# A language-model tower on one core: first-stage buffers in another order, left row slots loaded one by one, bias scaling in eight pieces, first expert split in the state stage

## The reference

```python
h = 16 * sum(where(in_range_i, table_i[idx] @ proj_i.T, 0))   # 4 tables, 256 wide
n = layernorm(h)
x = silu(conv3(n @ w1.T + w1_b))            # depthwise, along the 128 positions
y = ssm(x)                                  # h = h*sigmoid(A) + x*B; y = C.h + D*x
h = h + (y * silu(n @ v1.T + v1_b)) @ w2.T + w2_b
f = layernorm(h)
shared = silu(f @ sw1 + sb1) * (f @ sw3 + sb3) @ sw2 + sb2
experts = sum over 2 hashed experts of gelu(f @ w1[e] + b1[e]) @ w2[e] + b2[e]
out = h + (shared + experts / 2) / 2
```

## Time and profile before

| | us |
|---|---|
| median of 3 runs (lowest, highest) | 440.92 (440.53, 441.39) |
| the profiled execution | 442.19 |
| its span, first to last instruction | 440.3 |
| PE busy | 400.3 (91%) |
| DVE, ACT, POOL busy | 272.8, 242.9, 212.6 |
| mean granted TensorE clock | 0.984 |

### The profile page before, as it was taken

The page is one execution under the profiler, slowest core; times in us unless marked ns, Lnnn a source line. Parts: engine busy times, 40 slices in busy tenths (PEclk is TensorE's granted clock), DMA queues, the critical chain, the costliest instruction groups (busy, mean ns, idle before and its releaser), DMA issues.

```text
span 440.3 us, 8454 instructions
## 1 busy us (share of the span) xinstructions
PE 400.3 (91%) x2880; PEld 352.4 (80%) x2880; DVE 272.8 (62%) x607; ACT 242.9 (55%) x435; POOL 212.6 (48%) x236
## 2 busy tenths in 40 slices
PE   3878999899997785899999999999999999998996
PEld 2767888788677774698898998988988988887885
DVE  6558998889756577565556465565564554655333
ACT  4576778778877345644544635635635535535442
POOL 6569999831006456557347237247247336333000
PEclk9999999999998988899999999999999999999999
DMA  2433121249699983100121111201201301100101
GB/s 63 143 111 131 49 61 56 69 129 308 196 302 297 237 293 104 67 0 20 59 68 48 44 55 48 58 38 48 85 10 48 95 0 48 48 0 0 49 0 48
DMA packets 32779, 38.86 MB, mean 88 GB/s; under 512 B 3461, under 2 KB 29027, under 8 KB 32624
## 3 DMA queue, kind: packets, MB, share of 16 engines
q1 hardware_dynamic: 29616, 32.99, 24.3%
q0 software_dynamic: 3136, 5.52, 4.2%
HBM read 34.56 MB, written 8.65 MB: 98 GB/s over the span
## 4 chain that ended last, share of the span: by engine, by line
PE 62%; DVE 16%; POOL 6%; ACT 6%; issue 5%; DMA 3%; SPq 1%; DVEq 0%; ACTq 0%; POOLq 0%
PE ps L1140 20%; PE ps L1141 19%; PE ps L1142 19%; DVE hid_lo L1073 3%; DMA h_in<-h_rows_dram 2%; DVE stat L951 2%; DVE catT_lo L944 1%; POOL bias_e L646 1%; POOL bias_e L645 1%; PE ps L1259 1%; PE ps L1178 1%; DVE act_out L1067 1%; ACT act_out L845 1%; DVE x_mid L1004 1%; DVE rstd L978 1%
## 5 line engine op out<-in xcount | busy, mean ns | idle before, releaser
L1073 DVE SCALAR_TENSOR_TENSOR hid_lo<-act_out,hid_hi 128x512 fp32r<-128x512 f32 x64 | 54.4, 851 | 57.5 <-ACT hid_hi L858 57.5
L845 ACT ACTIVATE act_out<-ps,vec 128x512 f32<-128x512 f32 x32 | 22.1, 689 | 90.3 <-PE ps L1142 90.3
L1067 DVE SCALAR_TENSOR_TENSOR act_out<-ps,vec,act_out 128x512 f32<-128x512 f32 x32 | 24.0, 751 | 55.5 <-ACT act_out L845 55.5
L675 POOL TENSOR_TENSOR h_sb<-h_sb,bias_e 128x256 f32<-128x256 f32 x32 | 24.5, 769 | 53.4 <-DVE h2n L964 53.4
L1141 PE MATMUL ps<-h2nT_lo,sw_hi 128*128 128x512 f32 x128 | 50.0, 391 | 0.0
L1142 PE MATMUL ps<-h2nT_hi,sw_lo 128*128 128x512 f32 x128 | 50.0, 391 | 0.0
L1140 PE MATMUL ps<-h2nT_hi,sw_hi 128*128 128x512 f32 x128 | 49.9, 390 | 0.0
L668 POOL TENSOR_TENSOR zc_lo<-v_sb,zc_hi 128x256 fp32r<-128x256 f32 x32 | 28.8, 903 | 34.4 <-ACT zc_hi L835 34.4
L849 ACT ACTIVATE act_out<-ps,vec 128x512 f32<-128x512 f32 x32 | 22.0, 689 | 40.5 <-PE ps L1142 40.3
L858 ACT ACTIVATE hid_hi<-act_out 128x512 fp32r<-128x512 f32 x64 | 39.7, 622 | 0.0
L528 POOL DMA_INDIRECT cat<-table_dram,x_ids x32 | 35.1, 1097 | 8.3 <-issue 5.9
(11 more groups left out here) (133 smaller groups left out, 1260.9 us busy)
## 6 DMA issues: line engine op xcount, KB each, us to landing
toep_l<-kernel_rows_dram SPq DMA_DIRECT2D x14, 512.0 KB, 9.3
toep_r<-kernel_rows_dram SPq DMA_DIRECT2D x12, 512.0 KB, 6.9
h_rows_dram<-h_ring SPq DMA_DIRECT2D x32, 128.0 KB, 1.8
h_in<-h_rows_dram SPq DMA_DIRECT2D x8, 512.0 KB, 4.4
stage<-w_e_dram POOLq DMA_DIRECT2D x7, 512.0 KB, 3.6
out_dram<-o_sb SPq DMA_DIRECT2D x7, 512.0 KB, 3.2
bias_e<-rows_dram SPq DMA_DIRECT2D x1, 1024.0 KB, 7.2
toep_r<-kernel_rows_dram SPq DMA_DIRECT2D x4, 256.0 KB, 7.9
```

What stands on the lines that cost most here:

```text
L675: nc.gpsimd.tensor_tensor(at, at, bias_e[:, bass.ds(e, 1), :].rearrange("p o c -> p (o c)"), ALU.add).then_inc(h2_biased, 1)
L845: nc.scalar.activation(act_out[:, n % 4, :], ps[bank][:, :], ACT.Silu, bias=vec[:, C_SB1 + j:C_SB1 + j + 1]).then_inc(act_done, 1)
L1067: nc.vector.scalar_tensor_tensor(act_out[:, n % 4, :], ps[bank + 1][:, :], vec[:, C_SB3 + j:C_SB3 + j + 1], act_out[:, n % 4, :], ALU.add, ...
L1073: nc.vector.scalar_tensor_tensor(hid_lo[:, n % 4, :], act_out[:, n % 4, :], 0.5 if kind == SHARED else 0.25, f32(hid_hi[:, n % 4, :]), ALU ...
```

## The change

The order of the buffers on the left side is changed: `cat`, `k_row`, `abar`, `catT`, `proj` now come first, so that each 8 KB slot for rows lies over buffers that are last used at different times. `ex0` and `ex1` change places, so that `ex1` and `stage` lie clear of what the first stage uses. SP's order in the last group is written out, with a wait for just what a slot needs; the bias loads move ahead; the first expert's load (`piece_in(1)`) goes ahead of load 10, its hi part (ACT) into q = 4 of the state stage, its lo part (POOL) ahead of the mixer bias. The bias scaling is cut into a row and eight pieces, each behind a `cat_hi` of group 1.

```diff
-    x_ids = sb(mem_a, "x_ids", [P, GROUPS, RES], I32, L)
-    mask = sb(mem_a, "mask", [P, GROUPS, RES], F32, L)
     cat = sb(mem_a, "cat", [P, RES, CAT], F32, L)
+    k_row = sb(mem_a, "k_row", [P, YLEN, 2, 2], F16, L)
+    abar = sb(mem_a, "abar", [P, 7, HALVES * STATES], F32, L)
     catT_hi = sb(mem_a, "catT_hi", [P, 2, KC, P], F32R, L)
     catT_lo = sb(mem_a, "catT_lo", [P, 2, KC, P], F32R, L)
-    hn = sb(mem_a, "hn", [P, 4, D], F32, L)
     proj_hi = sb(mem_a, "proj_hi", [P, KC, D], F32R, L)
     proj_lo = sb(mem_a, "proj_lo", [P, KC, D], F32R, L)
+    hn = sb(mem_a, "hn", [P, 4, D], F32, L)
     h_ring = sb(mem_a, "h_ring", [P, 4, D], F32, L)
...
+    x_ids = sb(mem_a, "x_ids", [P, GROUPS, RES], I32, L)
+    mask = sb(mem_a, "mask", [P, GROUPS, RES], F32, L)
...
-        sp.dma_start(bias_row[:, 0:1, :], bass.AP(rows.tensor, D, [[0, P], [D, 1], [1, D]])).then_inc(rows_in, 16)
-        sp.dma_start(bias_e[:, :, :], bass.AP(rows.tensor, 2 * D, [[0, P], [D, RES], [1, D]])).then_inc(rows_in, 16)
-        with sp.Fori(1, GROUPS - 1) as i:
+            if r == 5:
+                sp.dma_start(bias_row[:, 0:1, :], bass.AP(rows.tensor, D, [[0, P], [D, 1], [1, D]])).then_inc(rows_in, 16)
+                sp.dma_start(bias_e[:, :, :], bass.AP(rows.tensor, 2 * D, [[0, P], [D, RES], [1, D]])).then_inc(rows_in, 16)
+        for i in range(1, GROUPS - 1):
             for r in range(RES):
                 h_store(i, r)
-        for r in range(RES):
-            h_store(GROUPS - 1, r)
-            if r == 1:
-                sp.wait_ge(k_out, 16)
-                sp.wait_ge(wv_lo_done, 2)
-            if r == 1 + TRIGHT:
-                sp.wait_ge(w_lo_done[1], 1)
-            if 2 <= r < 2 + TRIGHT:
-                toep_load(r - 2)
-
+        last = GROUPS - 1
+        h_store(last, 0)
+        sp.wait_ge(k_out, 16)
+        sp.wait_ge(wv_lo_done, 2)
+        toep_load(0)
+        toep_load(1)
+        h_store(last, 1)
+        toep_load(2)
+        h_store(last, 2)
+        sp.wait_ge(w_lo_done[1], 1)
+        toep_load(3)
+
+        h_store(last, 3)
+        sp.wait_ge(cat_tr, RES * last + 6)
+        toep_load(4)
+        h_store(last, 4)
+        h_store(last, 5)
+        sp.wait_ge(emb_done, RES * last + 7)
+        toep_load(5)
+        h_store(last, 6)
+        h_store(last, 7)
+        toep_load(6)
         sp.wait_ge(hn_turned, 4 * GROUPS)
-        sp.wait_ge(catT_lo_done, RES * GROUPS)
         for s in range(4):
             sp.wait_ge(h_stored[s], 16 * 2 * GROUPS)
-        for q in range(TRIGHT, NQ):
-            if q == TRIGHT + 4:
-                sp.wait_ge(mm_done, 8 * (GROUPS - 1))
-            if q >= TRING:
-                sp.wait_ge(ssm_done, 2 * (q - TRING + 1))
+        toep_load(7)
+        sp.wait_ge(mm_done, 8 * last)
+        toep_load(8)
+        toep_load(9)
+        sp.wait_ge(mm_done, 8 * GROUPS)
+        piece_in(1)
+        for q in range(TRING, NQ):
+            sp.wait_ge(ssm_done, 2 * (q - TRING + 1))
             toep_load(q)
...
-        piece_in(1)
         h_load(1, 1)
...
-        pool.wait_ge(bias_scaled, 2)
+        pool.wait_ge(bias_scaled, 1 + RES)
...
+        piece_lo(1)
         pool.wait_ge(rows_in, 48)
         add_w2_bias(0, 1)
         add_w2_bias(1, 1)
-        piece_lo(1)
...
+            if isinstance(i, int) and i == 1:
+                scale_bias(r)
+
+        def scale_bias(e):
+
+            if e == 0:
+                act.wait_ge(rows_in, 32)
+                nc.scalar.mul(bias_row[:, 0, :], bias_row[:, 0, :], 0.5).then_inc(bias_scaled, 1)
+            nc.scalar.mul(bias_e[:, e, :], bias_e[:, e, :], 0.25).then_inc(bias_scaled, 1)
...
-            if q == 1:
-                act.wait_ge(rows_in, 32)
-                nc.scalar.mul(bias_row[:, 0, :], bias_row[:, 0, :], 0.5).then_inc(bias_scaled, 1)
-                nc.scalar.mul(bias_e[:, :, :].rearrange("p e c -> p (e c)"), bias_e[:, :, :].rearrange("p e c -> p (e c)"),
-                              0.25).then_inc(bias_scaled, 1)
             for bank in range(2):
                 act.wait_ge(ssm_done, 2 * q + bank + 1)
                 nc.scalar.copy(y_at(q, bank), y_part(q, bank, 1)).then_inc(y_low, 1)
-        act.wait_ge(ssm_done, 2 * NQ)
-        piece_hi(1)
+            if q == 4:
+                piece_hi(1)
```

More of the change, by code:

```diff
@@ L132, in _tower @@
     wv_lo = sb(mem_a, "wv_lo", [P, 2, HALVES, D], F32R, L)
-    abar = sb(mem_a, "abar", [P, 7, HALVES * STATES], F32, L)
-    k_row = sb(mem_a, "k_row", [P, YLEN, 2, 2], F16, L)
+    x_ids = sb(mem_a, "x_ids", [P, GROUPS, RES], I32, L)
+    mask = sb(mem_a, "mask", [P, GROUPS, RES], F32, L)
     mem_a.close()
@@ L143, in _tower @@
     zc_lo = sb(ctx, "zc_lo", [P, GROUPS, HALVES, P], F32R, L)
-    ex1_hi = sb(ctx, "ex1_hi", [P, 2, BLK], F32R, L)
-    ex1_lo = sb(ctx, "ex1_lo", [P, 2, BLK], F32R, L)
+    ex0_hi = sb(ctx, "ex0_hi", [P, 2, BLK], F32R, L)
+    ex0_lo = sb(ctx, "ex0_lo", [P, 2, BLK], F32R, L)
     h_in = sb(ctx, "h_in", [P, 2, GROUPS, D], F32, L)
@@ L150, in _tower @@
     sw_lo = sb(ctx, "sw_lo", [P, 6, BLK], F32R, L)
-    ex0_hi = sb(ctx, "ex0_hi", [P, 2, BLK], F32R, L)
-    ex0_lo = sb(ctx, "ex0_lo", [P, 2, BLK], F32R, L)
+    ex1_hi = sb(ctx, "ex1_hi", [P, 2, BLK], F32R, L)
+    ex1_lo = sb(ctx, "ex1_lo", [P, 2, BLK], F32R, L)
     stage = sb(ctx, "stage", [P, 4, BLK], F32, L)
```

## The result

| | before | after |
|---|---|---|
| median of 11 runs each (lowest, highest) | 441.04 us (440.53, 442.88) | 444.53 us (442.30, 445.58) |
| ratio, 95% interval | | 1.0064, 1.0049 to 1.0079 |
| the profiled execution, its span | 442.19, 440.3 | 443.65, 442.0 |

The change made the kernel 0.64% slower (2.8 us by the ratio, 3.5 by the medians); forecast was 441.0, with a range to 443.2. The measured median lies above that range, and it stays above it when only the 2.8 us of the ratio are added to the 440.92 that the forecast started from (443.7).

A forecast was written before the change was run, and what follows sets the result against it. Bounds: the ACT-DVE-POOL chain while the pipeline fills, PE's instruction blocks fetched over a full DMA in the state stage, then `zc_lo` on POOL. Gains -4.2 - 0.6 + 2.5 + 2.2 = -0.1 us gave 441.0 us, range 437.2 to 443.2.

The forecast's parts named there:

- Bias load and scaling: Group 1: ACT waits 3.0 us for the bias behind `catT_hi` (1,0), plus scalings; 4.2 us lost, bounds 2.1 and 7.0.
- Bias sums on POOL: Tail before the state stage: 17 sums beside four DVE convolution instructions at 0.15 us each; 0.6 us lost, from 0 to 1.5.
- State stage and what is behind it: State stage 2.5 us shorter (bounds 1.5 and 7.2); then `h_sb` 2.2 us sooner, with `ex_lo` and `h_in` sums off the path.
- The `y_sb` wait: State stage before q = 3: PE's 1.25 us wait, held by ACT's bias scaling, was to go.
- the first two blocks: State stage: late instruction blocks of 256, fetched by DMA, that PE waits for; expected at 141.8 and 149.9 us.
- The third: State stage: the third instruction block, late before at 159.04 us, was to be late no more, as rows are in by then.
- a lower bound: Behind the state stage: gain of only 1.2 in place of 2.2 us if POOL's fourth `zc_lo` delays the first rstd.
- One line of the prediction: End of the state stage: from the second block at 149.9 us PE needs 5.5 us to the last one, given as 156.4.
- The early loads: Left slots' rows loaded one by one, all landed before the state stage; worth 0 alone, since PE never waited for rows.
- Rival 3: Slower, 29%: block intervals stay (stage +1.5 us), bias (-5.0) and DVE contention (-0.9) cost in full; 443.1 us.
- One of the named signs: Sign that the forecast is right: PE's first state matmul comes near 135 us, in place of 130.41 before.

The follow-up runs named there:

- e3: The changed kernel with the bias loads behind store (0,1) in place of (0,5): 440.79 us, ratio 0.9982 to the kernel before.
- e9: The changed kernel run once more, unaltered: profiled span 443.7 us, with a bias wait of 4.25 us.
- e10: The changed kernel run again, unaltered, as a second sample: profiled span 442.5 us, with a bias wait of 3.44 us.
- e7: The changed kernel with the bias part undone and left and right slots loaded as late as before: 439.89 us, ratio 0.9967 to the kernel before.
- e2: The kernel before with the bias part alone (early loads, pieces in group 1, sums after POOL's group 3): 444.93 us, ratio 1.0074.
- e1: The changed kernel with its bias part undone, early row loads and early first-expert split kept: 439.76 us, ratio 0.9960 to the kernel before.
- e6: The kernel before without the row loads of q = 10 to 15, some outputs wrong: 437.71 us, ratio 0.9907.

## Why the prediction was wrong, by its steps

**Bias load and scaling: -4.2 us forecast, 3.8 measured** as the mean of A over three profiles each. The mechanism and the place were right, and the size nearly: bias due at 31.0, landed at about 30.1, 31.7 and 32.2. The wait was 3.3 us in the mean (3.0 forecast). The other 0.5 us appeared only together with the wait, and no run takes them apart; I had 1.2 for the scalings, which without a wait cost 0.1 (e3). ACT had room for nine short instructions, but not for a wait.

**Bias sums on POOL: -0.6 us forecast, 1.9 measured, and this is the step that failed.** The bound, 1.5, did not hold it either. Two things were wrong in it. The first is what was counted: two pairs of convolution steps, at 118.90 and 124.69. But by the prediction's own times the sums start at 111.9, so the pair at 112.95 and DVE's norm at 111.94 stand beside them too. In the changed kernel the first pair ends 4.35 us after the last `rstd` began, 3.27 before, and the next pair begins 1.0 us late: more than half of the 1.9 us is lost there. The second is the price: 0.15 us an instruction, the median lengthening of a stretch in which POOL did a mixture of work. In the tail POOL does nothing but sums, back to back, and the second step took 1.108 us in the median in place of 0.752, the first up to 1.28. The rule of the Trainium skill that I set beside the row ("SBUF — State Buffer", Who interferes with whom) was right that the two engines contend. Its upper end of 3.0 us was not reached: POOL's sum went from 0.74 to 1.06 too, so both sides were stretched by some 0.3 to 0.5 us, and neither waited for a whole instruction of the other.

**State stage and what is behind it: +2.5 and +2.2 forecast, 1.6 and 1.9 measured, and 0.4 lost behind `h_sb`.** This is the second part of the miss, 1.2 us in C and 0.4 in D. Of the 1.2, 0.8 is the measure and not the change: the sum was made against a profile of before whose C was 0.8 us above the mean of three. From that profile the forecast was a C of 33.8; the changed kernel has 34.2 in the mean. The `y_sb` wait went as forecast, and so did the first two blocks: due 11.4 and 19.5 us after the first state matmul, they came at 11.1 to 11.3 and 19.2 to 19.7. The third was to be late no more; it was late in two of three profiles (1.25 and 0.28 us) and gone in the third, which is also the one with the shortest stage. In the first profile the last rows came 0.4 us late as well, at 160.0: 24.7 us after the stage began, where I had reckoned 18.9 from their bytes alone, and the DMA share was 1.01 up to 160. That profile's turns then ran partly at the lower clock (0.77 and 0.50 from 162 to 166 us), behind the last wait. The 0.4 us in D is POOL's `rstd` behind its fourth `zc_lo`, which the prediction had named as a lower bound. One line of the prediction does not add as written: 149.9 and 5.5 are 155.4, not 156.4. The 6.5 us that its result takes are near the 6.7 that e9 and e10 needed there.

**The early loads were forecast at 0 by themselves**, and e7 shows no gain (0.3 us, give or take 1.0).

**Why the gains did not reach the loss.** Two edits each took much of C when alone, against the mean of 37.72: taking the bias out of the stage 3.0 us (e2), and the early split of the first expert 2.1 without and 3.2 with the early loads (e7, e1). Together they were worth 3.5. The overlap lies behind the last state matmul: e2 gained 1.9 us there, e1 2.1 and both together 1.9. My reading is that both free the same thing, POOL ahead of the first `zc_lo`; no run takes it apart further. Against the 3.5 stood 5.7 us in A and B, not 4.8. Put together, the span is 2.6 us worse than forecast: 1.3 from B, 1.2 from C, 0.4 from D, less 0.4 from A. With 3.8 + 1.9 - 3.5 + 0.4 = 2.6 in place of 0.1 the forecast would have been 443.5. Rival 3 had the right side, the right place (ACT behind `catT_hi` of (1,0)) and nearly the right time, 443.1, but for partly other reasons: it put 0.9 on DVE, and 5.0 on the bias load.

One of the named signs came true by luck. The first state matmul was to come near 135, and came at 135.26: the wait of that execution was 0.7 us shorter than forecast, and the sums on POOL cost 1.3 us more.

## What to carry to other kernels

Work that is moved off a short, full stage lands somewhere: before moving it, look at whether the engine there has queued behind it what the others wait for, and whether its operands collide with what the neighbour does in the chain; here the two together cost 5.7 us, and one character (an earlier load) and one wait (later sums) turned a kernel 0.6% slower into one 0.7% faster. When work is put beside another engine's, count every instruction of the neighbour in that stretch, not only those of one kind. Two cures for one lateness don't add. A single profile can be a microsecond off the mean in one stage (C of before: 38.50, 37.35, 37.31); a forecast within 0.2% needs marks from several.

## What the runs showed of the hardware

PE stood still inside a stream of matmuls without a wait of its own, every 252 counted instructions plus a few waits, while the DMA share was about 1, and not at all in the same stretch at a share of 0.17 (e6). The page of the Trainium skill on the fetch ("Runtime: NRT & Kernel Launch", Instruction fetch mechanics: blocks of 256 by DMA, mostly hidden) fits the period. That it is hidden does not hold here, where it cost 3.6 to 4.2 us in each profile of before. That the blocks are what is waited for is inferred from the period and from e6, not seen.

DVE's steps and POOL's sums, each with two inputs in the memory, stretched each other: DVE from 0.752 us to 1.108 in the median and 1.28 at most, POOL from 0.74 to 1.06. DVE's norm, which reads one large tile, was stretched as well, from 0.73 to 1.28 us for its two instructions together. Over the whole of B this came out the same within 0.02 us in five profiles. Six loads of 1 MB took a tenth longer to issue than six of 0.75 MB with equal packet counts, at 354 against 276 GB/s. An SP issue of a 128 KB broadcast, just behind stores, took 0.43 us in some executions and 1.4 to 2.1 in others.

The granted clock did not follow the waits in a fixed way. Behind the longest issue wait (2.1 to 3.0 us) it fell to between 0.50 and 0.77 in five of the six profiles of the two kernels; in the first profile of the changed kernel it stayed at 1.00 from 153 to 160 us and fell only behind the third wait.
